# Moving layer-norm statistics between stages, a bias as three products, wider pad packets and an earlier table read in a transformer block with experts

## The reference

```python
x = x + attention(layernorm(x))      # 16 heads, features elu + 1, linear attention, out @ wo.T + bo
x = x + ffn(layernorm(x))

# attention, per batch and head
qf, kf = elu(q) + 1, elu(k) + 1
out = (qf @ (kf.T @ v)) / (qf @ sum(kf) + 1e-6)

# ffn
top_vals, top_idx = top_k(x @ router_w.T, 2)        # 16 experts
moe = sum over the 2 of sigmoid(top_val) * expert(x)  # (silu(x @ gate) * (x @ up)) @ down, width 128
return moe + (silu(x @ sg.T) * (x @ su.T)) @ sd.T     # the shared expert, width 256
```

## Time and profile before

| | before |
|---|---|
| median of 3 runs | 274.89 us (272.03 to 275.07) |
| profiled execution, its own time | 275.04 us |
| its span | 273.2 us |
| TensorE (PE) busy | 226.7 us, 83% |
| VectorE (DVE) busy | 172.7 us, 63% |
| ScalarE (ACT) busy | 119.1 us, 44% |
| GpSimd (POOL) busy | 139.5 us, 51% |

### The profile page before, as it was taken

How to read it: one execution, slowest core, us unless ns; L and a number is a source line. 1 busy time by engine, 2 the same in 40 slices (tenths; PEclk the granted TensorE clock), 3 DMA queues, 4 the chain that set the end, 5 groups by cost and what they waited for, 6 DMA issues and landing times.

```text
span 273.2 us, 5157 instructions
## 1 busy us (share of the span) xinstructions
PE 226.7 (83%) x1306; PEld 174.3 (64%) x1307; DVE 172.7 (63%) x677; ACT 119.1 (44%) x316; POOL 139.5 (51%) x148
## 2 busy tenths in 40 slices
PE   7695975888988988869997979979979979979910
PEld 2364654767767756645895868858768758758810
DVE  2633688869889888557436656646646646732595
ACT  2634473476576370213222545545535535641200
POOL 0000000375777776767710777777777777777000
PEclk9977999599999997997999999999999999997975
DMA  7960000011111111112934332332332332210798
GB/s 234 411 259 1 2 0 1 21 51 39 49 50 51 59 49 52 51 43 73 171 56 116 97 100 82 105 106 87 102 100 83 106 105 86 88 35 0 247 388 287
DMA packets 25705, 27.63 MB, mean 101 GB/s; under 512 B 4656, under 2 KB 21305, under 8 KB 25558
## 3 DMA queue, kind: packets, MB, share of 16 engines
q1 hardware_dynamic: 17606, 15.90, 19.7%
q0 software_dynamic: 4608, 8.47, 9.2%
q10 hardware_dynamic: 3472, 3.04, 3.6%
HBM read 15.70 MB, written 12.73 MB: 104 GB/s over the span
## 4 chain that ended last, share of the span: by engine, by line
PE 52%; DVE 24%; issue 8%; DMA 6%; ACT 4%; POOL 2%; SPq 1%; POOLq 1%; DVEq 0%
PE pKVN L1010 8%; PE pZ L1004 6%; PE pQ L1004 6%; DMA ZB<-results 4%; PE pT L996 4%; PE pKV L831 4%; PE pKVN L870 4%; PE pN L821 3%; PE pT L999 3%; DVE ZB L518 3%; PE pZ L903 2%; DVE c_stat L478 2%; PE pKVN L821 2%; DVE a_stat L478 2%; PE pT L807 2%
## 5 line engine op out<-in xcount | busy, mean ns | idle before, releaser
L320 POOL DMA_INDIRECT routed<-ZB,ROWS x64 | 61.5, 961 | 75.6 <-DVE ROWS L614 56.3
L329 POOL DMA_INDIRECT results<-Y,XS x80 | 77.8, 972 | 37.1 <-issue 19.2
L699 DVE COPY xhT<-pT 128x256 f32<-128x256 f32 (+1 forms) x83 | 34.4, 414 | 16.7 <-PE pT L999 15.6
L1010 PE MATMUL pKVN<-WF,xhT 128*128 x160 | 34.8, 299 | 1.5 <-ACT Y L423 1.5
L1010 PEld LDWEIGHTS pKVN<-WF,xhT 128*128 128x128 f32 x160 | 26.4, 189 | 15.0 <-issue 13.1
L423 ACT ACTIVATE Y<-pKVN,XS 128x128 f32<-128x128 f32 x80 | 29.3, 367 | 4.9 <-PE pKVN L1010 2.1
L996 PE MATMUL pT<-CN,XS 128*128 128x128 f32 x80 | 22.9, 286 | 8.2 <-issue 6.7
L1004 PE MATMUL pZ<-WF,xhT 128*128 x80 | 24.3, 385 | 0.0
L1004 PE MATMUL pQ<-WF,xhT 128*128 x80 | 24.0, 382 | 0.0
L870 PE MATMUL pKVN<-WA,XNT 128*128 128x256 f32 x64 | 20.1, 470 | 4.2 <-ACT XNT L367 4.2
L710 DVE TENSOR_TENSOR sh_h<-pN,sh_s 128x512 f32<-128x512 f32 x16 | 11.0, 690 | 19.6 <-PE pKV L831 12.2
(11 more groups left out here) (134 smaller groups left out, 422.7 us busy)
## 6 DMA issues: line engine op xcount, KB each, us to landing
XS<-routed SPq DMA_DIRECT2D x80, 65.0 KB, 1.8
ZB<-results SPq DMA_DIRECT2D x8, 512.0 KB, 6.7
WF<-w_ffn SPq DMA_DIRECT2D x1, 3456.0 KB, 13.6
X<-x SPq DMA_DIRECT2D x8, 256.0 KB, 5.1
out<-X ACTq DMA_DIRECT2D x8, 256.0 KB, 4.6
results<-Y,XS POOLq DMA_INDIRECT x80, 2.2
routed<-ZB,ROWS POOLq DMA_INDIRECT x64, 2.3
routed<-pad SPq DMA_DIRECT2D x11, 65.0 KB
```

The costliest lines, as they stand in the source:

```text
L320: nc.gpsimd.indirect_dma_start(routed, bass.IndirectOffsetOnAxis(ap=ROWS[:, q, t, k:k + 1], axis=0), Z[:, q, t, k, :], None).then_inc(scat ...
L329: nc.gpsimd.indirect_dma_start(results, bass.IndirectOffsetOnAxis(ap=XS[:, j, D:D + 1].bitcast(U32), axis=0), Y[:, j, :], None, bounds_che ...
L699: nc.vector.tensor_copy(xhT[:, j % 2, a:b, :], pXH[:, a:b, :]).then_inc(s_xhT, 1)
L1010: nc.tensor.matmul(pY, xhT[:, (j + 3) % 2, 1, :], WF[:, 2 * EXP_DIM:][:, bass.ds(w, D)], start=True, stop=True).then_inc(s_D, 1)
```

## The change

- Bias: one row of bo is loaded, split into three tiles of one row by five operations (no scaling by the identity), now ahead of unit 1. `output` issues three products of one row, and its two holds are gone. The waits for the parts and for `tri` move from TensorE's step 0 to their first use.
- Statistics: unit 2 ahead of VectorE's loop, its newton stays in step 0; units 3 and 4 both in step 1 directly behind `mask(0)`, their newtons at the end of step 1. ScalarE's `rstd` of units 3 and 4 both in step 1, ahead of the copy of attT.
- Pads: the pad tile is 16 partitions of 8 rows, so that each pad block is 16 pieces of 4160 B instead of 128 of 520 B. The 17th goes out behind the loads. SP reads the table's entries and then waits for pads.
- TensorE's first holds wait for the memset of V alone (s_ones), which stands behind that of `pad`; the skip marks of `pad` have a semaphore of their own (s_pad).

```diff
@@ -98,13 +99,9 @@
         WF = sb("WF", [P, F_ALL])
         CN = sb("CN", [P, C_ALL])
         TOK = sb("TOK", [P, NQ * QUAD * TOP_K], U32)
-        bo_row = sb("bo_row", [PARTS, D])
-        bo_high = sb("bo_high", [PARTS, D], BF16)
-        bo_mid = sb("bo_mid", [PARTS, D], BF16)
-        bo_low = sb("bo_low", [PARTS, D], BF16)
-        bo_rest = sb("bo_rest", [PARTS, 2, D])
-        bo_sum = sb("bo_sum", [PARTS, 2, D])
-        bo_parts = sb("bo_parts", [PARTS, D], BF16)
+        bo_row = sb("bo_row", [1, D])
+        bo_rest = sb("bo_rest", [1, 2, D])
+        bo_part = [sb(f"bo_part{i}", [1, D], BF16) for i in range(PARTS)]
         ones = sb("ones", [P, P], BF16)
         tri = sb("tri", [P, P], BF16)
         eps = sb("eps", [P, 1])
@@ -149,7 +146,7 @@
         gate_e = sb("gate_e", [P, QUAD, TOP_K])
         gate_1 = sb("gate_1", [P, QUAD, TOP_K])
 
-        pad = sb("pad", [P, ROW])
+        pad = sb("pad", [PAD_PARTS, P // PAD_PARTS, ROW])
         pad_at = sb("pad_at", [1, EXPERTS], I32)
         nb_a = sb("nb_a", [EXPERTS, P], I32)
         nb_b = sb("nb_b", [EXPERTS, P], I32)
@@ -195,7 +192,7 @@
         s_cn, s_tok, s_wa, s_wf = sem("s_cn"), sem("s_tok"), sem("s_wa"), sem("s_wf")
         waited = sem("waited")
         s_x = [sem(f"s_x{q}") for q in range(NQ)]
-        s_ones, s_tri, s_bo, s_parts = sem("s_ones"), sem("s_tri"), sem("s_bo"), sem("s_parts")
+        s_ones, s_pad, s_tri, s_bo, s_parts = sem("s_ones"), sem("s_pad"), sem("s_tri"), sem("s_bo"), sem("s_parts")
         a_stats, a_aggr, a_rstd, a_norm = sem("a_stats"), sem("a_aggr"), sem("a_rstd"), sem("a_norm")
         a_ln, a_y, a_n1, a_n2 = sem("a_ln"), sem("a_y"), sem("a_n1"), sem("a_n2")
         a_shift = sem("a_shift")
@@ -241,10 +238,6 @@
 
             return q if q < 2 else q // 2 + 1
 
-        def stats(s):
-
-            return 0 <= s < 3
-
         def wait_apart(eng, semaphore, count):
 
             eng.wait_ge(semaphore, count)
@@ -263,7 +256,8 @@
         def pads(eng, first, count):
 
             for at in values(eng, pad_at, first, count, EXPERTS * REGION - P):
-                eng.dma_start(routed[bass.ds(at, P), :], pad[:, :]).then_inc(t_pads, 16)
+                eng.dma_start(routed[bass.ds(at, P), :].rearrange("(p r) c -> p r c", p=PAD_PARTS),
+                              pad[:, :, :]).then_inc(t_pads, 16)
 
         block = ctx.enter_context(nc.Block())
 
@@ -277,10 +271,11 @@
             sp.dma_start(WF[:, :], w_ffn).then_inc(s_wf, 16)
 
 
+            sp.wait_ge(s_pad, 1)
+            sp.dma_start(routed[EXPERTS * REGION:EXPERTS * REGION + P, :].rearrange("(p r) c -> p r c", p=PAD_PARTS),
+                         pad[:, :, :]).then_inc(t_pads, 16)
             sp.wait_ge(t_pad, 2)
             pads(sp, 0, EXPERTS - ACT_PADS)
-            sp.dma_start(routed[EXPERTS * REGION:EXPERTS * REGION + P, :], pad[:, :]).then_inc(t_pads, 16)
-            sp.wait_ge(t_pads, 16 * (EXPERTS + 1))
 
             def places(it):
                 return values(sp, table_b, it * BODY + LEAD, BODY, EXPERTS * REGION_BLOCKS)
@@ -295,6 +290,7 @@
 
             sp.wait_ge(t_table, 2)
             at = places(0)
+            sp.wait_ge(t_pads, 16 * (EXPERTS + 1))
             for s_ in scat:
                 sp.wait_ge(s_, 16 * QUAD * TOP_K * NQ // 2)
             load(0, at)
@@ -389,13 +385,16 @@
                     act.wait_ge(a_rq, s + 1)
                     wait(act, a_qf, s)
                     nc.scalar.activation(eq[:, :], rq[:, :], ACT.Exp, scale=-1.0).then_inc(a_eq, 1)
+                if s == 0:
+                    rstd(a_mv, a_rs, a_aggr, a_ln, a_y, 2, unit(2))
+                if s == 1:
+                    rstd(a_mv, a_rs, a_aggr, a_ln, a_y, 3, unit(3))
+                    rstd(a_mv, a_rs, a_aggr, a_ln, a_y, 4, unit(4))
                 if att_:
                     q = s - 1
                     act.wait_ge(b_T, q + 1)
                     wait(act, b_wo, q)
                     nc.scalar.copy(attT[:, :], pAT).then_inc(b_aT, 1)
-                if stats(s):
-                    rstd(a_mv, a_rs, a_aggr, a_ln, a_y, s + 2, unit(s + 2))
                 if last:
                     q = s - 2
                     act.wait_ge(c_top, q + 1)
@@ -468,10 +467,10 @@
             nc.vector.memset(chosen_all[:, :], 0.0)
             nc.vector.memset(table_e[0:1, 0:LEAD], 0).then_inc(t_table, 1)
             nc.vector.memset(eps[:, :], LN_EPS)
-            nc.vector.memset(pad[:, :], 0.0).then_inc(t_pad, 1)
+            nc.vector.memset(pad[:, :, :], 0.0).then_inc(t_pad, 1)
             nc.vector.memset(V[:, :, :, D:D + 1], 1.0).then_inc(s_ones, 1)
             dve.wait_ge(t_pad, 1)
-            nc.vector.memset(pad[:, D:D + 1].bitcast(U32), SKIP).then_inc(s_ones, 1)
+            nc.vector.memset(pad[:, :, D:D + 1].bitcast(U32), SKIP).then_inc(s_pad, 1)
 
             def bn_stats(src, at, stat, stats, tiles=range(QUAD)):
                 for t in tiles:
@@ -641,6 +640,9 @@
                     bn_aggr(c_stat, c_mv, c_stats, c_aggr, s - 2)
                 if att_:
                     mask(s - 1)
+                if s == 1:
+                    statistics(3)
+                    statistics(4)
                 if last:
                     newton1(c_mv, c_rs, c_y, c_n1, s - 2)
                     newton2(c_rs, c_n1, c_n2, s - 2)
@@ -652,9 +654,11 @@
                 if this:
                     features_k(s, s % 2)
                     features_q(s, s % 2)
-                if stats(s):
-                    statistics(s + 2)
-                    newton(s + 2)
+                if s == 0:
+                    newton(2)
+                if s == 1:
+                    newton(3)
+                    newton(4)
                 if last:
                     route(s - 2)
 
@@ -662,32 +666,27 @@
 
                 dve.wait_ge(s_bo, 16)
                 with nc.allow_low_precision("three bfloat16 parts that add up to the float32 number"):
-                    nc.vector.tensor_copy(bo_high[:, :], bo_row[:, :]).then_inc(s_parts, 1)
+                    nc.vector.tensor_copy(bo_part[0][:, :], bo_row[:, :]).then_inc(s_parts, 1)
                     dve.wait_ge(s_parts, 1)
-                    nc.vector.tensor_tensor(bo_rest[:, 0, :], bo_row[:, :], bo_high[:, :], ALU.subtract).then_inc(s_parts, 1)
-                    nc.vector.tensor_scalar(bo_sum[:, 0, :], bo_high[:, :], ident[0:PARTS, 0:1], None, ALU.mult).then_inc(s_parts, 1)
+                    nc.vector.tensor_tensor(bo_rest[:, 0, :], bo_row[:, :], bo_part[0][:, :], ALU.subtract).then_inc(s_parts, 1)
                     dve.wait_ge(s_parts, 2)
-                    nc.vector.tensor_copy(bo_mid[:, :], bo_rest[:, 0, :]).then_inc(s_parts, 1)
+                    nc.vector.tensor_copy(bo_part[1][:, :], bo_rest[:, 0, :]).then_inc(s_parts, 1)
+                    dve.wait_ge(s_parts, 3)
+                    nc.vector.tensor_tensor(bo_rest[:, 1, :], bo_rest[:, 0, :], bo_part[1][:, :], ALU.subtract).then_inc(s_parts, 1)
                     dve.wait_ge(s_parts, 4)
-                    nc.vector.tensor_tensor(bo_rest[:, 1, :], bo_rest[:, 0, :], bo_mid[:, :], ALU.subtract).then_inc(s_parts, 1)
-                    nc.vector.scalar_tensor_tensor(bo_sum[:, 1, :], bo_mid[:, :], ident[0:PARTS, 1:2], bo_sum[:, 0, :],
-                                                   ALU.mult, ALU.add).then_inc(s_parts, 1)
-                    dve.wait_ge(s_parts, 5)
-                    nc.vector.tensor_copy(bo_low[:, :], bo_rest[:, 1, :]).then_inc(s_parts, 1)
-                    dve.wait_ge(s_parts, 7)
-                    nc.vector.scalar_tensor_tensor(bo_parts[:, :], bo_low[:, :], ident[0:PARTS, 2:3], bo_sum[:, 1, :],
-                                                   ALU.mult, ALU.add).then_inc(s_parts, 1)
+                    nc.vector.tensor_copy(bo_part[2][:, :], bo_rest[:, 1, :]).then_inc(s_parts, 1)
 
             statistics(0)
             dve.wait_ge(s_cn, 16)
             nc.vector.tensor_copy(tri[:, :], CN[:, C_TRI:C_TRI + P]).then_inc(s_tri, 1)
             newton(0)
+            bias_parts()
             statistics(1)
             newton(1)
-            bias_parts()
             dve.wait_ge(s_tok, 16)
             nc.vector.tensor_copy(Z[:, :, :, :, D].bitcast(U32),
                                   TOK[:, :].rearrange("p (q t k) -> p q t k", q=NQ, t=QUAD))
+            statistics(2)
             for s in range(NQ + 3):
                 step(s)
 
@@ -807,7 +806,7 @@
                     nc.tensor.matmul(bank[:, :], ones[:, :], ones[:, :].unsqueeze(1).to_broadcast([P, QUAD, P]),
                                      start=True, stop=True)
 
-            pe.wait_ge(s_ones, 2)
+            pe.wait_ge(s_ones, 1)
             hold(pZ, 24)
             pe.wait_ge(s_cn, 16)
             pe.wait_ge(s_wa, 16)
@@ -912,8 +911,10 @@
 
             def output(q):
 
-                nc.tensor.matmul(pO[:, :], ones[0:PARTS, :], bo_parts[:, :].unsqueeze(1).to_broadcast([PARTS, QUAD, D]),
```

(10 more changed lines are left out.)

2 lines of the change are left out of this document (1 added, 1 removed).

## The result

| | before | changed |
|---|---|---|
| median | 274.98 us, 4 runs (272.03 to 276.11) | 265.72 us, 4 runs (264.95 to 266.1) |
| profiled execution, its span | 275.04, 273.2 us | 265.36, 263.5 us |
| mean granted clock of TensorE over the span (1.00 is full speed) | 0.937 | 0.941 |

The ratio is 0.9699, with an interval of 0.9627 to 0.9771. The kernel is 9.3 us faster. The forecast was 13.0 us (262.0 us); the time lies inside the range of 258.5 to 267.5.

What follows compares the result with a forecast made beforehand. Whatever precedes the first result scatter at 150.31 us was taken to move the end one for one, with GpSimd's scatters closing the chain. Gains of 14.3 us less 1.3 for the clock gave 13.0, so 262.0 us, range 258.5 to 267.5.

Steps and rivals of the forecast that it cites:

- Terms 1 and 2: Quad 0's keys: early bias parts start them 1.9 us sooner, at full clock they take 1.73 us; sum 3.3 us.
- Term 3: Unit 2's statistics hidden in VectorE's idle time before the loop; quad 1's keys start another 3.0 us sooner, sum 6.3 us.
- Term 4: Units 3 and 4 in VectorE's step 1 idle time; attend1(0) at 23.0 instead of 29.69 us, sum 6.7 us.
- Terms 5, 6, 7: Rest of step 1, step 2 without unit 4, step 3 without TensorE starvation: 2.1, 3.3 and 2.2 us, sum 14.3 us.
- Term 8: TensorE's clock falls elsewhere: 1.3 us given back, one early stretch and one late; bounds nothing and 2.2 us twice.
- Term 9: Three bias products replace one and two holds per output: 0 us, bounds 0.1 us a step either way.
- Term 10: Pads in fewer packets land sooner and table loads precede SP's wait, covered by shared work: 0, bounds 0 and 0.3 us gain.
- Term 11: Larger pad memset at the start takes 0.8 to 1.4 us, ends by 2.4 us, delays nothing.
- A: The forecast: all statistics units hidden or nearly, early steps at full clock, 259 to 264.5 us; chance 0.66.
- B: Clock falls in many steps because one-row bias products replace 128-row holds: 264.5 to 269 us; chance 0.17.
- D: GpSimd's scatters, 10.1 us a step, bind if steps get shorter and take back 1 to 3 us; chance 0.06.
- E: Statistics collide with features and stay on the path; only terms 1, 2 and 7 come: 5.5 us, 269.5 us; chance 0.09.

Runs made afterwards that it cites:

- e11: Changed kernel with bias parts made behind unit 1 again and TensorE's step 0 waiting for them; slower chip, 340.15 us, ratio 0.9657.
- e13: Changed kernel run again unedited, as yardstick on another chip: 266.84 us, ratio 0.9766 to the kernel before.
- e1: Changed kernel with the pad tile back at 128 partitions of one row, 128 packets of 520 B a block: 266.09 us, ratio 0.9725.
- e15: Changed kernel with SP waiting for all pads ahead of the table's register reads again: 266.89 us, ratio 0.9736.
- e8: Changed kernel with 14 holds of 128 rows instead of 3 ahead of the drain's last transposes: 265.56 us, ratio 0.9667.
- e14: Changed kernel with pad rows in every eighth partition, 12 drain holds instead of 3, 6 holds at each later expert-loop turn: 260.2 us, ratio 0.9514.
- e2: Changed kernel with two holds of 128 rows back ahead of each output, three bias products kept: 267.96 us, ratio 0.9775.
- e12: Kernel before with only the statistics of units 2, 3 and 4 moved, nothing else of the change: 265.54 us, ratio 0.9611.
- e10: Changed kernel with spread pad rows, 12 drain holds and 6 holds at each later expert-loop turn, on the slower chip: 337.57 us, ratio 0.9586.
- e9: Changed kernel with every hold cut to one row, same 512 columns and count; slower chip, 347.9 and 349.2 us, ratio 0.9867.
- e4: Changed kernel with the same 4160 B pad packets, but from partitions 0, 8 ... 120: 265.65 us, ratio 0.9698.
- e3: Changed kernel with statistics of units 2, 3 and 4 back at the end of VectorE's steps 0 to 2; slower chip, 351.52 us, ratio 0.9951.

## Why the prediction was right or wrong, by its own steps

- **What bounds the kernel**: right. What came ahead of the first scatter moved the end nearly one for one: 10.6 us there (150.31 to 139.70), 9.7 at the end. The first scatter itself was forecast near 137.3 us; the clock and the pads put it at 139.70.
- **Terms 1 and 2**, keys(0) at 11.2 us and at full clock: 11.13 us, 1.99 us long, where I had 1.73. Without the early bias it is 12.28 us (e11). The 1.4 us for the clock were 3.17 less 1.73 us. That keys(0) would get the full clock was my estimate, with a pause of 0.5 us ahead of them, and no run shows that term; in the changed kernel the holds end at 11.10 us (10.29 + 0.81) and keys(0) start at 11.13, and 3.17 us became 1.99, 1.2 us less.
- **Term 3**, keys(1) at 17.2 us (20.5 less the 3.3 gained already): 17.18.
- **Term 4**, attend1(0) at 23.0 us straight behind a bn_aggr: 22.31, and it is straight behind it. That the two units would be the last wait by 1.5 us was my estimate, with keys(1) at the full clock, and no run shows that term; in the changed kernel the last numerators are done at 21.56 us (L885, 20.42 + 1.14), so the units are the last wait by 0.75 us.
- **Terms 5, 6, 7**, residuals at 27.2, 36.9 and 47.3 us: 26.39, 36.12 and 46.38. The sum of 14.3 us measured 15.2. The early part was forecast 0.9 us too small. The second and third are each 0.8 and 0.9 us early because the first is.
- **Term 8**, given back by the clock, 1.3 us: this is the term that was mis-sized. Clock and timing took about 4.0 us: 0.3 from the third to the eighth residual, 0.7 in the drain, 2.1 in the shared work, 0.9 in the loop. The 0.9 may be no effect of the change: the loop of four profiles of this kernel or nearly this one (changed, e13, e1, e15) took 123.80 to 124.70 us. The upper bound of 4.4 held the 4.0, but by luck: it was made of two early steps, and the early steps lost nothing. The step that was wrong is the place: I looked for the late stretch in a steady step, at the price of one (0.3 us at 102 us; in the changed kernel the stretch at 85.7 to 92.6 us made its step 11.41 us instead of 10.42, 1.0 us), and not at the shared work behind the drain, which is TensorE alone, so that the lower clock counts in full: 4.4 of the low 10.3 us lie behind the counts. Keys took 3.64 us at 0.50 and 1.89 at 1.00, about twice as long, so I estimate the loss at half of the 4.4 us, 2.2 us; measured are the 2.1 above. With 11 and 9 more full-row holds in the drain (e8, e14) the clock stayed up there, and also with two holds ahead of each `output` (e2, e12); on the slower chip it did not (e10).
- **Term 9**, three bias products at 0: the products themselves cost nothing in the steps at full clock (10.26 us twice from 36 to 57 us and 10.42 twice up to 77 us, against 10.37 and 10.59 before). What goes with them may cost: e12, which keeps the old product and the holds, had no low stretch from 15.8 to 210 us, and in e9 products of one row did not raise the clock. But the kernel before had the holds as well and fell to 0.50 at 102.0 and 122.5 us, and e2, with the holds back beside three one-row products, was not faster. How much of term 8 is due to the rows of these products, and how much to the phase in which the low stretches happened to fall, is not settled.
- **Term 10**, pads and table at 0: right for the table (e15), wrong for the pads. I took 16 packets instead of 128 to land sooner; they took 12.1 us instead of 9.95. And the sentence that the six pads on ScalarE cost nothing that TensorE waits for failed: they held ScalarE for 4.25 us and TensorE for 1.30. The cost was 1.4 to 1.5 us in this profile (e1, e4), outside the bounds that I gave, and it is not a fixed price (0.23 to 1.91 us of idle time of TensorE in the five profiles). The bytes of a packet were my measure; the partitions that they come from weren't in the sum.
- **Term 11**, the memset: 0.93 us, ended by 2.10 us, hidden; it lies between the bounds of 0.8 and 1.4 us. The 0.07 us that the lower bound takes as fixed is the length of the memset of V, 8 elements a partition (before, L472).
- **Net**: 15.2 - 4.0 - 1.5 = 9.7 us of span. The forecast had 14.3 - 1.3 = 13.0. The gain and its mechanism were right; 4.2 us were missing in terms 8 and 10, and an early part that came out 0.9 us better than forecast made up for some of them. Without that piece of luck the time would be about 266.6 us, still inside the range.
- **Rivals**: A was the right one in kind, but the time of 265.7 us lies above its band (264.5 us) and in B's. B's mechanism exists (e9), but whether it is part of term 8 is open; its form, lower clock in many steps, didn't come: only the stretch at 85.7 to 92.6 us lies in the steps. C (the low clock in steps 2 to 7 and the drain, 276 us or more), D and E didn't happen: scatters never bound the steps, and nothing collided with the features. No run shows C's price of 2.2 us at every one of seven places; of the steps only the one at 85.7 us was slowed in the changed kernel, by 1.0 us.
- **Signs of being wrong**: one of the three came, if only just. Between slices 7 and 17 there are two low tenths as before, but 5 and 5 where before has 5 and 7, and the second stretch goes on into slice 18. The other two did not come: VectorE has no long waits in steps 1 and 2, and the end of the shared work still sets the first block.

## What to carry to other kernels

Work that no one needs yet belongs into a stretch where the trace shows its engine idle: moving three units of statistics there gave the whole gain (e12, e3). When a gain ahead of a dense TensorE stage is predicted, ask how TensorE enters that stage: a low stretch that reached into it cost about 2 us here. Filling the idle stretch just before it with full-row holds kept the clock up in two profiles (e8, e14), but not on the slower chip (e10), so try it and look. A packet isn't cheap because it is large: with its source rows in neighbouring partitions a packet of 4160 B took 0.62 us here, with the rows in every eighth partition 0.185 to 0.190, so try to spread them. Slow transfers in the queue of an engine that feeds TensorE can hold that engine up, here ScalarE for 4.25 us; whether sending all pads from SP would avoid it, no run shows.

## What the runs showed of the hardware

- DMA packets of 4160 B from 16 neighbouring partitions took 0.62 us each, from every eighth partition 0.185 to 0.190 us (changed, e4). No run here shows why.
- While the slow pads were under way, register reads of two numbers on ScalarE's queue took up to 3.34 us (785 ns in the median before), and the ten pad DMAs of SP took 10.04 us to issue instead of 5.66. With the same packets from spread partitions the reads took at most 0.97 us (e4). So in these runs an engine whose queue had slow transfers under way was held up itself.
- 24 gapless products of 512 columns and one row ran for 10.4 us at 0.43 us each (e9); with 128 rows the 24 took 7.29 us in e10 and 7.84 in the changed kernel, the first ones 0.43 us apart and the last 0.22. The granted clock is shown as 1.00 over the first 12 us in both, so ahead of the first recorded change the durations say it, not that column. So 10.4 us of products of one row without a gap did not bring the faster pace here.
- The same idle stretch of 2.2 us of TensorE in the drain was followed by a low clock in six profiles on the faster chips (0.50 from 122.5 us on before, from 105.9 to 106.6 in changed, e1, e4, e13, e15) and not in two (e2, e12). Where holds filled the stretch no low clock followed until 250.5 us (e8) and 244.9 us (e14).
- The same kernel, the one before, took 275 to 276 us on two chips and 354 us on a third. The profiles of e14 and e10, one kernel on two chips, are 75.6 us apart: 26.2 from the first to the eighth residual (steps of up to 16 us), 3.3 to the counts, 8.6 in the shared work and 37.6 in the loop. The scatters of routed rows take 0.96 us in both, and up to the second residual the two profiles agree.
